# Gathering all 28 rows of a pair of groups with GpSimd in the attention passes of a four-layer graph network

## The reference

```python
def _gat_layer(h, src, dst, Ws, Wd, a_s, a_d, bias):
    N = h.shape[0]
    xs = (h @ Ws).reshape(N, H, C)          # H = 4 heads, C = 32
    xd = (h @ Wd).reshape(N, H, C)
    alpha_s = jnp.sum(xs * a_s, axis=-1)
    alpha_d = jnp.sum(xd * a_d, axis=-1)
    e = jax.nn.leaky_relu(alpha_s[src] + alpha_d[dst], NEG_SLOPE)
    emax = jax.ops.segment_max(e, dst, num_segments=N)
    ex = jnp.exp(e - emax[dst])
    alpha = ex / (jax.ops.segment_sum(ex, dst, num_segments=N)[dst] + EPS)
    return jax.ops.segment_sum(xs[src] * alpha[:, :, None], dst, num_segments=N).reshape(N, H * C) + bias
```

## Time and profile before

| | us |
|---|---|
| median of 3 runs (5045.73 to 5054.8) | 5050.2 |
| span of the profiled execution | 6621.7 |
| busy VectorE (DVE) | 3946.6 |
| busy TensorE (PE, matmuls) | 3707.6 |
| busy GpSimd (POOL) | 2812.1 |
| busy ScalarE (ACT) | 2597.0 |
| the three attention passes, from the first gather to the last update | 1231.45, 1269.70, 1259.11 |

### The profile page before, as it was taken

The page is one execution under the profiler, slowest core; times in us unless marked ns, Lnnn a source line. Parts: engine busy times, 40 slices in busy tenths (PEclk is TensorE's granted clock), DMA queues, the critical chain, the costliest instruction groups (busy, mean ns, idle before and its releaser), DMA issues.

```text
span 6621.7 us, 64379 instructions
## 1 busy us (share of the span) xinstructions
PE 3707.6 (56%) x17056; PEld 1903.0 (29%) x17056; DVE 3946.6 (60%) x10821; ACT 2597.0 (39%) x6428; POOL 2812.1 (42%) x2909
## 2 busy tenths in 40 slices
PE   7998856554554564555544754555533323323799
PEld 3443523222222232322322322322321111111444
DVE  8998846555555555655554655655557777776511
ACT  5885143332332333323323332333326666665300
POOL 0001265545444645445446545445425555555100
PEclk8999878777777777777776777777756666665899
DMA  4445323222222222223222322222215555556266
GB/s 166 154 154 213 129 81 95 90 80 82 88 80 78 73 86 85 86 75 90 80 87 61 99 80 84 87 77 87 83 41 221 221 221 221 221 221 223 76 224 236
DMA packets 323828, 817.06 MB, mean 123 GB/s; under 512 B 80799, under 2 KB 239551, under 8 KB 308676
## 3 DMA queue, kind: packets, MB, share of 16 engines
q1 hardware_dynamic: 201244, 594.04, 23.3%
q0 software_dynamic: 92336, 200.10, 12.3%
q10 hardware_dynamic: 29944, 19.32, 1.1%
HBM read 350.23 MB, written 462.98 MB: 123 GB/s over the span
## 4 chain that ended last, share of the span: by engine, by line
DVE 32%; another core or an unknown queue 22%; PE 13%; ACT 11%; issue 11%; DMA 1%; POOL 0%; ACTq 0%; DVEq 0%; POOLq 0%
DVE big L1773 10%; PE psT L1038 5%; DVE big L1689 5%; DVE big L1763 5%; ACT hT L879 3%; DVE big L1713 3%; PE psT L1182 1%; PE psY L1182 1%; PE psY L1262 1%; PE psY L1232 1%; DVE big L1769 1%; DVE top_b L1744 1%; ACT psT L918 1%; DVE m_b L1749 1%
## 5 line engine op out<-in xcount | busy, mean ns | idle before, releaser
L690 POOL DMA_INDIRECT big<-table,src_win x2660 | 2560.0, 962 | 2379.8 <-DVE big L1773 988.9
L895 ACT ACTIVATE psH<-d_b 128x60 f32<-128x60 f32 x168 | 37.6, 224 | 2270.2 <-DVE d_b L1755 1903.8
L1773 DVE SCALAR_TENSOR_TENSOR big<-big,keep_win 128x132 f32<-128x132 f32 x2184 | 779.2, 357 | 126.4 <-DVE big L1773 37.8
L1204 PE MATMUL psS<-big,hT 128*128 128x384 bf16 x1400 | 352.0, 429 | 790.6 <-DVE hT L1698 421.4
L866 ACT ACTIVATE hT<-src_bc,node_c 128x640 bf16<-128x640 f16 x840 | 621.4, 815 | 300.8 <-remote 190.9
L1182 PE MATMUL psT<-big,hT 128*128 128x408 bf16 x1200 | 388.5, 387 | 463.9 <-DVE big L1713 377.8
L1182 PE MATMUL psY<-big,hT 128*128 128x408 bf16 x1200 | 388.6, 387 | 383.5 <-DVE big L1713 358.6
L1182 PE MATMUL psT<-big 128*128 128x408 bf16 x1800 | 496.3, 340 | 65.1 <-DVE big L1689 43.2
L1182 PE MATMUL psY<-big 128*128 128x408 bf16 x1800 | 494.9, 339 | 29.4 <-issue 29.4
L871 ACT ACTIVATE hT<-hT 128x3200 bf16<-128x3200 bf16 x168 | 482.2, 2870 | 5.4
L1204 PEld LDWEIGHTS psS<-big,hT 128*128 128x128 bf16 x1400 | 169.3, 124 | 973.2 <-issue 934.7
(11 more groups left out here) (368 smaller groups left out, 7758.0 us busy)
## 6 DMA issues: line engine op xcount, KB each, us to landing
rows<-big SPq DMA_DIRECT2D x112, 1792.0 KB
rows<-big SPq DMA_DIRECT2D x168, 952.0 KB
big<-A_d SPq DMA_DIRECT2D x17, 6400.0 KB, 19.3
A_d<-big SPq DMA_DIRECT2D x396, 200.0 KB, 1.9
big<-table,src_win POOLq DMA_INDIRECT x2660
big<-A_d SPq DMA_DIRECT2D x7, 1600.0 KB, 7.3
src_bc<-pe_src_d ACTq DMA_DIRECT2D x84, 128.0 KB
table<-big SPq DMA_DIRECT2D x15, 350.0 KB
```

The lines of the kernel that those rows point to most:

```text
L690: pool.indirect_dma_start(out=rows[:, k, 0:p.table_w], out_offset=None, in_=table, in_offset=bass.IndirectOffsetOnAxis(ap=src_win[:, s, k: ...
L1204: ins = nc.tensor.matmul(psS[:, 0:3 * D].rearrange("p (c w) -> p c w", c=3), is_src[:, t, 0:P], table_s[:, t, :, 0:D], start=(n == 0), sto ...
L1773: v.scalar_tensor_tensor(state[:, k, 0:GATW], prev[k][:, 0:GATW], kw[:, 0, k:k + 1], rows[:, k, 0:GATW], ALU.mult, ALU.add).then_inc(chain ...
```

## The change

In an attention pass TensorE fetches nothing any more: GpSimd gathers 14 rows for every slot. The one-hots, the broadcasts and the three parts of the table are left out in these passes, on ScalarE and on VectorE. The PNA pass keeps its one fetched row a pair. The helper functions stay in the file and aren't called there.

```diff
@@ class Pass
-        self.by_pe = {GAT: 2, PNA: 0}[kind]
+        self.by_pe = {GAT: 0, PNA: 0}[kind]
@@ def dma_steps(self, s)
-        return self.by_dma - s % 2
+        return self.by_dma - (s % 2 if self.pairs else 0)
@@ ScalarE, start of a pass
-                            if b >= 2 and b != 6:
-                                high(b - 2 if b < 6 else 4)
-                    for b in range(NB):
-                        middle(b)
@@ ScalarE, group(rnd, s, final)
                         nc.scalar.activation(cw_p, d_b[:], ACT.Exp).then_inc(exp_rdy, 1)
-                        q = rnd * (SLOTS // 2) + s // 2
-                        if s % 2 == 0 and q + 2 < p.groups // 2:
-
-                            act.wait_ge(is_src_rdy, p.halves0 + 2 * q + 2)
-                            act.wait_ge(is_src_v_rdy, p.halves0 + 2 * q + 2)
-                            broadcast(q + 2)
-                        if s % 2 == 0 and q + 1 < p.groups // 2:
-                            own_hots(q + 1, 1)
-                        if s % 2 and q + 2 < p.groups // 2:
-                            own_hots(q + 2, 0)
@@ VectorE, start of a pass
-                for b in range(NB - 1 if p.kind == PNA else 0, NB + 2):
+                for b in range(NB - 1, NB + 2) if p.kind == PNA else []:
                     split(b)
```

## The result

The changed kernel takes 5541.73 us (median of 4 runs, 5540.16 to 5544.23) where the kernel before took 5049.07 us on the same chip (4 runs, 5045.73 to 5054.8): **1.0971 times as long, with a 95% interval of 1.0958 to 1.0984**. The forecast was 5533 us.

The account below looks back on a forecast made before the run. GpSimd's gathers were taken to bound an attention pair. Three passes of 140 added gathers at 1.225 us, less 10.6 us per start, gave +483 us on 5050.2: 5533 us, range 5340 to 5620.

Parts of the forecast that it names:

- GpSimd bounds a pair of before, VectorE 2.5 us behind: Attention pair before the change, in the runs: GpSimd needs 29.1 us for 23 gathers, VectorE 26.6 us without its wait.
- The 0.35 us for the changes of slot: GpSimd in an attention pair: about 0.35 us on top of the gathers for changing slots.
- the pair of 35.3 us: Attention pair after the change: GpSimd with all rows gathered takes 35.3 us, while VectorE needs 19 us.
- What is removed is worth nothing: Attention pairs: work taken off VectorE (some 7.5 us), ScalarE (14 us) and TensorE (23.8 us busy) saves nothing in steady pairs.
- 1.249 us per gather, lowered to 1.225 by the budget: Each of 420 added GpSimd gathers: 1.249 us in the trace, taken as 1.225 us in the runs.
- The budget: Whole kernel before, rebuilt without false waits: 5166 us at 1.249 a gather, 5036 at 1.20; the runs' median lies between.
- 10.6 us less at each start, contention not counted: Start of each attention pass: GpSimd's idle 8.6 us and an estimated 2 us go, -32 us in all.
- The span near 5880 us: Profiled execution after the change: false wait gone, a pass 1007 us instead of 1253, so the span falls by 739 us.
- VectorE's wait of about 8 us in each group: Sign in the profile after: VectorE waits about 8 us per group for a gather's landing, ahead of the first addition.
- B: Rival on GpSimd's gathers: only 0.945 us each in the runs, so about 5040 us, no change; chance 0.04.
- A: Rival: VectorE's 18.93 us wait for TensorE's fetched rows is real in the runs, so the change wins, 4484 us; chance 0.10.
- The rule on blocking: Skill page: two-port VectorE instructions and GpSimd's block each other fully; removed one-hots would return 5.8 us a pair, about 5055 us.

Follow-up runs that it names:

- experiment 1: The kernel before with two gathers fewer per attention pair (21 instead of 23), TensorE's fetch kept: 4889.05 us beside 5054.83, ratio 0.9675.
- experiment 5: The kernel before and the changed kernel measured and profiled again, unaltered: before 5054.39 us; changed 5536.52 us beside 5051.21, ratio 1.0959.
- experiment 2: The kernel before with all 28 rows of a pair gathered too, TensorE's fetch, one-hots and reductions still done: 5553.06 us, ratio 1.0989.
- experiment 3: The changed kernel with five rows of a pair left out, so 23 gathers and no TensorE fetch: 5029.1 us, ratio 0.9957 to the kernel before.
- experiment 7: The changed kernel with each attention gather fetching half of the bytes, 70 numbers instead of 140: 5549.21 us, one run, beside 5536.52.

## Why the prediction was right, and which of its steps were not

**The forecast held**: 5533 us where 5541.73 was measured, inside the range of 5340 to 5620. Step by step:

- *GpSimd bounds a pair of before, VectorE 2.5 us behind.* Right. Shown by experiment 1 (26.45 us a pair when GpSimd is relieved) and by GpSimd's 5 us of waits in 778 in experiment 5. The 29.1 us hold for the steady part; with the first pairs at VectorE's pace the mean is 28.46. The 0.35 us for the changes of slot in it are not there: in the second pass of the first profile of after GpSimd is idle for 239.0 us before its 784 gathers, 0.305 us each, and the pair of 35.3 us is 35.1. In the kernel before slowed gathers fill the place. It does no harm in the sum, where the 0.35 stands on both sides.
- *What is removed is worth nothing.* Right, by experiment 2: 11 to 17 us.
- *1.249 us per gather, lowered to 1.225 by the budget.* This is the term that was mis-sized. The cadence in the new profiles is 1.249 us, that of the earlier trace rows. At 1.249 the sum was +493 us, and +492.7 was measured on the first chip. On the second it was +485.3.
- *The budget.* It failed in the part outside the attention passes. I took ScalarE's false-looking waits out of the PNA pass, 218 us, and had 2861.4 - 218 = 2643 us left outside the attention passes. In the new profile the three passes, counted as in the earlier trace rows, take 835.0, 835.5 and 839.3 us (1773.1 to 2608.6 the second), so 5052.6 - 2509.8 = 2543 us are outside. Its PNA matmuls run from 3640.6 to 4537.9, 897 us, against 4964.3 to 6102.6, 1138 us, in the old: 241 us less, where I had taken 218; some 77 us more went from the stages around the passes, where I had taken nothing. The undisturbed rest was 100 us shorter than I made it, and I read those 100 us as cheaper gathers. That the median lay between my two sums said nothing of a gather.
- *10.6 us less at each start, contention not counted.* 10.7 us a pass in experiment 5, but of another make: GpSimd's wait for a window is 4.2 us in before's second pass, not 8.6, and slowed gathers are the rest. By the first profile of after it is 8.1, so that 10.7 meets 10.6 is luck. In the whole kernel experiment 3 gives 26 us for the three passes with 32 forecast.
- *The span near 5880 us.* Wrong by 340 us: it was 5539.8. It rested on the first profile's rest being that long in the next one too. The step that failed is the cause: I put the waits down to the recording, which would have stayed, and they come and go with the chip, as far as two such chips and four others show. The pair of 35.3 us is 966.3/27.5 = 35.1 here, and VectorE's wait of about 8 us in each group is there.

```profile
L1749 DVE TENSOR_TENSOR big<-big,psH x56: 2078/2078/2080, 1962.1 to 2928.4; 128x1848 f32<-128x1848 f32 x56
```

Of the rivals, B (a cheap gather) fell by the cadence and by experiment 7. A, the real wait, fell for the chips on which the kernel before takes 5050 us, and is true where it takes 6640: there the change gains 6%, not the 11% that rival A gave, since VectorE's starts are late in the new kernel too. The chance of 0.10 was for the wrong question, whether the wait is real; it should have been on which chip the time is taken. That the changed kernel was timed on one of the quick kind was no merit of the forecast. The rule on blocking falls for these instructions: the traces show 0.13 us more for a part of the gathers that coincide with a one-hot, and nothing for the others.

## What to carry to other kernels

Hold the span of a profile against the runs before reading any wait in it. If they differ by more than a per cent or so, bound every engine by its own instructions and cadence, take the waits out of all parts of the span, not only where they stand out, and ask for another profile on another chip. And when an engine is relieved, the gain ends at the next engine's pair, and it counts from the measured mean of a pass, not from the steady pair: two gathers fewer brought 2.0 us of 2.5, and moving one over to TensorE and VectorE brought those two to 28.5 us a pair and the kernel nothing. One gather more cost 1.0 us of 1.25, because the lighter fetch slowed GpSimd less.

## What I had not expected of the hardware

- A gather on GpSimd and a one-hot on VectorE that overlap cost the gather some 0.13 us in 29 of 121 cases and nothing in the others, and the one-hot nothing (392 ns beside 390).
- The same program took 5049 to 5056 us in four measurements (medians of 4 to 9 runs) and 6642 and 6714 us in two others, on two other chips (11 runs each), and the change turned from 1.096 into 0.9395 between them. In the long runs GpSimd's gathers kept their 1.249 us, the busy time of every engine stayed within 3% (changed kernel), and only the starts of VectorE's, ScalarE's and TensorE's instructions came late, those of VectorE in steps of 0.70 us.
- A gather of 128 rows costs GpSimd 1.249 us, 0.94 busy and 0.30 to the next, with 560 bytes a row and with 280 alike.
